# Smaller batches of gather steps between the dense tiles of a graph network on one core

## What is computed

```
def _tagconv(x, src, dst, norm, W, b):
    out = x @ W[0]
    h = x
    for k in range(1, K + 1):          # K = 3
        msg = norm[:, None] * h[src]
        h = jax.ops.segment_sum(msg, dst, num_segments=x.shape[0])
        out = out + h @ W[k]
    return out + b
h = relu(_tagconv(x, ..., W1, b1))
h = relu(_tagconv(h, ..., W2, b2))
x = _layernorm(x + _tagconv(h, ..., W3, b3))
```

## Time and profile before

| | |
|---|---|
| time, median of 3 runs | 1798.29 us (1796.39 to 1801.66) |
| span of the profiled execution | 1250.4 us |
| granted TensorE clock, mean | 0.993 |
| PE busy | 1224.4 us (98%) |
| POOL busy | 850.6 us (68%) |
| DVE busy | 629.7 us (50%) |
| ACT busy | 397.2 us (32%) |
| gather matmuls L1319 | 900, 58.8 us busy |
| fetches L942 | 837, 807.9 us busy |

### The profile page before, as it was taken

The page is one execution under the profiler, slowest core; times in us unless marked ns, Lnnn a source line. Parts: engine busy times, 40 slices in busy tenths (PEclk is TensorE's granted clock), DMA queues, the critical chain, the costliest instruction groups (busy, mean ns, idle before and its releaser), DMA issues.

```text
span 1250.4 us, 19518 instructions
## 1 busy us (share of the span) xinstructions
PE 1224.4 (98%) x7413; PEld 610.2 (49%) x7413; DVE 629.7 (50%) x1552; ACT 397.2 (32%) x916; POOL 850.6 (68%) x937
## 2 busy tenths in 40 slices
PE   5999999999999999999999999999999999999997
PEld 4655554444444444444444454444444544454444
DVE  7876664444455555433443345555433433345655
ACT  6676774422233331111221122222111111112222
POOL 8677775777477755776577657773777477747773
PEclk8999999999999999999999999999999999999999
DMA  5343443544255553444354435553444344435553
GB/s 182 111 124 107 115 124 101 156 135 135 79 142 157 146 126 104 131 130 125 108 156 132 122 97 150 149 149 94 131 130 128 102 129 130 131 92 151 153 162 93
DMA packets 110070, 160.05 MB, mean 128 GB/s; under 512 B 43719, under 2 KB 82225, under 8 KB 109970
## 3 DMA queue, kind: packets, MB, share of 16 engines
q0 software_dynamic: 40480, 110.54, 31.6%
q1 hardware_dynamic: 69416, 48.13, 12.8%
q10 hardware_dynamic: 74, 0.05, 0.0%
HBM read 120.51 MB, written 32.10 MB: 122 GB/s over the span
## 4 chain that ended last, share of the span: by engine, by line
PE 88%; POOL 5%; DVE 3%; issue 2%; ACT 1%; DMA 1%; POOLq 0%; DVEq 0%; ACTq 0%
PE pb L1405 65%; PE pb L1266 6%; POOL GB L942 4%; PE pb L1319 4%; PE pb L1268 3%; PE pb L1285 3%; PE pb L1161 2%; PE pb L1410 1%; PE pb L1291 1%; PE pb L1383 1%; PE pb L1194 0%; DVE V L1744 0%; POOL gT L825 0%; DMA GB<-vh,KS 0%; DVE gT L1503 0%
## 5 line engine op out<-in xcount | busy, mean ns | idle before, releaser
L942 POOL DMA_INDIRECT GB<-vh,KS x837 | 807.9, 965 | 371.2 <-issue 246.2
L1405 PE MATMUL pb<-V,A 128*128 128x512 f16 x4104 | 944.8, 379 | 0.0
L1405 PEld LDWEIGHTS pb<-V,A 128*128 128x128 fp8e4 x4104 | 395.3, 98 | 429.5 <-issue 5.2
L1789 DVE SCALAR_TENSOR_TENSOR pb<-pb,cst,t 128x256 f32<-128x256 f32 (+1 forms) x200 | 97.7, 488 | 357.8 <-ACT t L1120 357.8
L1120 ACT ACTIVATE t<-pb,cst 128x256 f32<-128x256 f32 (+1 forms) x224 | 105.2, 469 | 441.8 <-PE pb L1410 398.0
L1266 PE MATMUL pb<-Whl,gT 128*128 128x512 f16 x384 | 134.2, 380 | 1.2 <-DVE gT L1730 1.2
L1761 DVE SCALAR_TENSOR_TENSOR V<-V,pb 128x256 f16<-128x256 f16 (+1 forms) x200 | 83.8, 421 | 82.1 <-ACT V L1090 81.5
L1090 ACT ACTIVATE V<-pb 128x256 f16<-128x256 f32 (+1 forms) x200 | 75.9, 383 | 127.3 <-DVE pb L1789 127.2
L1268 PE MATMUL pb<-Whl,gT 128*128 128x256 f16 x384 | 104.7, 273 | 0.0
L1632 DVE TENSOR_REDUCE stat<-V 128x1 f32<-128x256 f16 x225 | 91.3, 412 | 0.2
L1780 DVE TENSOR_REDUCE ast<-A 128x1 f32<-128x610 uint8 x100 | 77.8, 778 | 0.0
(11 more groups left out here) (227 smaller groups left out, 687.8 us busy)
## 6 DMA issues: line engine op xcount, KB each, us to landing
vh<-V SPq DMA_DIRECT2D x216, 128.0 KB
GB<-vh,KS POOLq DMA_INDIRECT x837, 2.8
xr<-in_x SPq DMA_DIRECT2D x24, 128.0 KB, 3.0
out<-g SPq DMA_DIRECT2D x24, 128.0 KB, 1.9
xr<-in_W SPq DMA_DIRECT2D x22, 128.0 KB, 2.4
V<-in_xt SPq DMA_DIRECT2D x5, 512.0 KB, 6.1
gT<-w SPq DMA_TRANSPOSE x46
V<-in_xt SPq DMA_DIRECT2D x1, 640.0 KB, 3.8
```

The lines of the kernel that those rows point to most:

```text
L942: pool.indirect_dma_start(GB[:, slot, :], None, vh[vbuf[(L, k + 1)]][:, :], bass.IndirectOffsetOnAxis(ap=KS[:, p:p + 1], axis=0))\
L1405: mm = pe.matmul(acc[:, :], A8[:, a, t * P:(t + 1) * P], src[:, a, :], start=False, stop=(n == NT - 1), skip_group_check=True)
L1789: dve.scalar_tensor_tensor(hi, hi, cst[0:r, 1, t:t + 1], lt, ALU.mult, ALU.add).then_inc(S["s_d1"], 1)
```

## The change

The three tables get more entries. `FIRST` is as it was. A short hop had five batches of five steps (one whole tile each) and now has ten of two or three; a long one had six and now has eleven (the tail's five steps stay together). The number of steps, their order within a hop, their fetches and their slots are the same.

```
-STEPS = {4: 5, 8: 10, 11: 15, 15: 20, 19: 25}
+STEPS = {2: 2, 4: 5, 6: 7, 8: 10, 10: 13, 12: 15, 14: 18, 16: 20, 18: 23, 19: 25}
...
-LONGER = {2: 5, 5: 10, 8: 15, 12: 20, 15: 25, 18: 30}
-LAST = {4: 5, 8: 10, 11: 15, 15: 20, 18: 25}
+LONGER = {2: 5, 4: 8, 5: 10, 7: 13, 8: 15, 10: 18, 12: 20, 14: 23, 15: 25, 17: 28, 18: 30}
+LAST = {2: 2, 4: 5, 6: 7, 8: 10, 10: 13, 12: 15, 14: 18, 16: 20, 17: 22, 18: 25}
```

## The result

The changed kernel takes **1613.78 us** (median of four, 1608.82 to 1626.05) against 1797.83 us (1796.39 to 1801.66) for the kernel before beside it: a ratio of **0.8995, 95% interval 0.8952 to 0.9038**. The forecast was 0.40% slower, with 2 in 100 for faster. It is 10% faster.

What follows compares the result with a forecast made beforehand. PE's own sequence was taken to bound the kernel. Switches +7.9, removed waits -1.3 and new waits +0.6 gave +7.2 us on 1798.3, so 1805.5 us (0.40% slower), with an 8-in-10 range of 1802.0 to 1809.5.

Steps and rivals of the forecast that it cites:

- The 547.9 us around the span: Time outside the profiled span of 1250.4 us, taken as the same instructions in another order and left unchanged.
- PE's own sequence sets the time: Whole kernel: PE, busy 1224.4 of 1250.4 us and 88% of the chain, pays for whatever is added to it.
- The switches: PE changing between dense and gather form: 35 added batches at 0.21 us and 5 at 0.11 us, +7.9 us.
- the drain rule: Skill page's rule that changing tiling mode drains TensorE: 4.0 us for all 75 added switches; the prediction kept 7.9.
- The removed waits: PE's waits for blocks inside three batches of five, 0.4, 0.7 and 0.2 us, would go: -1.3 us.
- The new waits: Early batches at index 2 of hops (1,2) and (2,2) wait about 0.3 us each, long hops nothing: +0.6 us.
- POOL's side: Slots freed later do not hold POOL, and earlier blocks are worth nothing to a PE that is not waiting.
- the changed profile's tests: Next profile: PE busy and span up about 7 us, short batches 0.75 and 0.97 us, wait near 548 us gone.
- signs of being wrong: Span within 2 us of 1250.4, PE block waits over 3 us in all, or POOL waiting longer for L1319.
- The whole-tile batches wait more in ordinary runs than in the profiled one: Rival, short hops: twelve later tiles each waiting 0.7 us would save 8.4 us, result -0.5 us, 1797.8 us; chance 0.03.
- The cheap switch: Rival: each of 40 added batches costs only one side's 0.10 us, so +3.3 us, 1801.6 us; chance 0.12.
- Late blocks: Rival: early batches at index 2 wait for the longest landing, +4.2 us, so +10.8 us, 1809.1 us; chance 0.12.

Runs made afterwards that it cites:

- b0: The kernel before, unchanged, run again for a profile: 1251.29 us, beside 1251.75 us for the kernel before in its group.
- a0: The kernel after, unchanged, timed in three rounds against the kernel before, without the hold-up: 1262.97 us against 1251.70 us, ratio 1.0092.
- e4_longer: The kernel before with only the new table `LONGER` (two long hops get eleven batches), held up: 1767.61 us beside 1803.5 us.

## Why the prediction was wrong

**The step that failed.** "The 547.9 us around the span are the same instructions in another order, so I leave them." The profiled execution of b0 took 1251.29 us with a span of 1249.5. There was no time around the span: but for 1.8 us the 547.9 us were lost inside the timed executions, to a hold-up that the profiled one did not have (span 1801.7 us in the held-up run of before). The prediction forecast the plain execution and added the result to held-up times. In numbers: in held-up executions the kernel before loses 1797.8 - 1251.7 = 546.1 us, that after 1613.8 - 1263.0 = 350.8. The change takes 195.3 us of it away and costs 11.3 of its own, which makes the 184.0 us measured.

**What bounds the kernel.** "PE's own sequence sets the time" holds in plain executions. In held-up ones PE waits for nothing visible while POOL issues fetches fast.

**The switches.** +7.9 us for 40 batches at 0.21 and 0.11 us rests on 0.75 and 0.97 us for a short batch; a0 has 0.75 and 0.96. Against the drain rule of the Trainium skill (TensorEngine Tiling (Array Packing), section Key Properties) with 128 cycles for a pass (TensorE: Matmul & The Clock Gate, section Step-by-step: what each phase is for), an estimate of 4.0 us, the rows were right: the trace agrees that a change of form costs, and it costs about 0.10 us, twice that estimate.

**The removed waits.** -1.3 us was the share of one execution. In b0 the three batches take 1.63, 1.55 and 1.58 us, so 0.23 + 0.15 + 0.18 = 0.56 us over 1.40; in a0 these waits are gone, as forecast.

**The new waits.** +0.6 us was too little. In a0 the waits of hops (1,2) and (2,2) at index 2 are 0.28 and 0.27 us, as worked out, but in hop (0,0) the batches at indices 4 and 7 take 1.63 and 1.49 us, 0.65 and 0.52 more than a batch of three, where the prediction had put nothing. The last batches of two in the long hops took 1.08 and 1.07 us, 0.33 us above an undisturbed 0.75, each; there PE waits 0.26 us for DVE (L1798), not for a block. Together 7.9 - 0.6 + 0.6 + 1.2 + 0.7 = 9.8 of the 11.3 us; the last 1.5 us were not traced.

**POOL's side.** "POOL is not held" and "earlier blocks are worth nothing" asked only when blocks come. That the pattern of POOL's fetches could act on PE otherwise was not asked. Of the changed profile's tests, the first missed: PE busy up by 7.8 us in a0 (1231.4 against 1223.6), as forecast, but by 118.5 us in the execution measured. One of its signs of being wrong came true there too: POOL waits 233.4 us for L1319, where it had waited 11.3.

**The rivals.** "The whole-tile batches wait more in ordinary runs than in the profiled one" (0.03) had the side right and the premise that ordinary runs differ from the profiled one, but its mechanism, blocks that come late, and its 8.4 us were not what happened. The 547.9 us spoke for such a difference as loudly as a row can, and were read as overhead instead. The cheap switch is ruled out by a0 (0.75 and 0.96 us for undisturbed batches in all hops). Late blocks came in part, but in hop (0,0), not at index 2 of the two hops named.

## What to carry to other kernels

Before any row is used, set the time of the profiled execution beside its span and beside the timed runs; where they differ by more than a few us, the profile is of another kind of execution, and the range must reach as far as the gap. When PE shows gaps with "issue" inside a stream of matmuls whose inputs are long there, look at what the other engines issue in those us, here indirect DMAs back to back, and test it with a rest on that engine. In this kernel a producer that ran ahead in bursts cost more, in held-up executions, than one that was slower and even.

## What was not expected of the hardware, and what stays open

- Long series of indirect DMAs of 128 rows every 1.25 us from POOL went, in held-up executions, with PE starting one matmul per 0.7, 1.4 or 2.1 us, in place of one per 0.22. In runs of 18 and 24 fetches of after and e4_longer it begins 11 to 17 us into the run (first distance of over 0.5 us) and, where a pause of over 8 us follows, mostly ends 2.4 to 4.3 us behind it. At a mean of 1.51 us between fetches nearly all of it was gone. That it hangs on POOL's rate is shown by the rests; by what path the one holds up the other is open. The queues show no difference: the instruction queue q8 has 61 packets and 1.00 MB in both kinds, 1.08 us a packet in b0 and 1.05 in after, and in after none starts between 633.2 and 683.8 us, around the stretch shown above; the packets of queue q0, which has the bulk of the bytes, take 0.156 us in the mean in b0 and 0.154 in after. So slower transfers are not what the traces show.
- Other engines are late then too. In after PE waits 20.12 us for one scaling by ACT, which starts 19.7 us behind the last matmul ahead of it (PE's timeline, then ACT's):

```profile
281.26 0.27 PE L1410 MATMUL pb<-V,A 128*128 128x256 f16 x1
301.65 1.04 PE L1319 MATMUL pb<-GB,SG 128*32 128x512 f16 x8 [20.12 <-ACT pb L977]
```
```profile
300.94 0.66 ACT L977 ACTIVATE pb<-pb,cst 128x512 f32<-128x512 f32 x1 [8.48 <-remote]
```

In the stretch shown above the last matmul of a tile starts at 671.46 us, and its drain on an idle ACT at 682.95, 11.5 us later; at the end of the next tile, with POOL at rest, it is 0.3 us (688.05 and 688.36).

- The granted clock went to 0.5 in these stretches, so a stall costs more than its idle time: of the 363.7 us by which after's span exceeds a0's, 252.2 us are PE's idle time and 111.5 us its longer busy time, most of it from the half clock, by the estimate above.
- Traces of the two kinds differ in what they record. The landings of fetches are there in a plain one and missing in a held-up one (DMA issues of a0: out<-in, op, count, us to landing; then of after):

```profile
GB<-vh,KS POOLq DMA_INDIRECT x837, 2.8
```
```profile
GB<-vh,KS POOLq DMA_INDIRECT x837
```

The split is clean over all traces: those of the twelve plain executions hold 19,099 to 19,240 records of semaphore updates by DMAs, those of the eight held-up ones 5,809 to 8,264, from the same number of DMAs. Two things follow. "issue" and "remote" in a held-up trace can hide a releaser whose record is missing; the readings above rest on matmuls in the middle of a dense tile, whose inputs are long there. And a rival stays untried: that something outside the kernel, the recording included, loads what the engines' semaphores go through. Whether the missing records are a sign of what differs or only go with it was not tried. What makes an execution held up is open: the kernel before, unchanged, was plain in some groups and held up in others, and no edit here chose it.
